# Rounding by an integer tile in place of a large added constant, with the input buffer cut from two to one

## The reference, cut to what matters

```python
xn = layernorm(x)                        # x: [8, 4096, 1024], one batch row a core
x  = x + attn(xn) + ffn(xn)

def activation_quant(x):                 # int8 steps, one scale for each token
    scale = 127.0 / clip(max(abs(x), axis=-1), EPS, None)
    return clip(round(x * scale), -128, 127) / scale
def weight_quant(w):                     # -1, 0 or 1, one scale for the whole weight
    scale = 1.0 / clip(mean(abs(w)), EPS, None)
    return clip(round(w * scale), -1, 1) / scale
def bitlinear(x, w, b):
    return activation_quant(rmsnorm(x)) @ weight_quant(w).T + b
ffn  = lambda x: bitlinear(gelu(bitlinear(x, w1, b1)), w2, b2)
# attn: gated linear attention with decay, 16 heads of 64, then an RMS norm,
# a silu gate and the product with Wo
```

## Time and profile before

| What | Value |
|---|---|
| Median of 3 runs | 6116.22 us (6114.14 to 6116.5) |
| The profiled execution: time | 6119.08 us |
| The profiled execution: span of the slowest core (7) | 6117.5 us |
| Spans of the 8 cores | 6094.9 to 6117.5 us |
| Busy in the span: PE, DVE, ACT, POOL | 3221.6, 1884.1, 1217.1, 155.3 us |
| Chain that ended last: PE, DVE, issue, ACT, DMA, SP's queue | 37%, 24%, 13%, 10%, 9%, 6% |
| Granted TensorE clock, mean of each core | 0.699 to 0.701 of full speed |
| Phase A (from the first chunk to the barrier) | about 225 to 3550 us |
| Phase B's chunks | about 3600 us to the end |

### The profile page before, as it was taken

The page is one execution under the profiler, slowest core; times in us unless marked ns, Lnnn a source line. Parts: engine busy times, 40 slices in busy tenths (PEclk is TensorE's granted clock), DMA queues, the critical chain, the costliest instruction groups (busy, mean ns, idle before and its releaser), DMA issues.

```text
span 6117.5 us, 54514 instructions; the slowest of 8 cores (6094.9 to 6117.5 us)
## 1 busy us (share of the span) xinstructions
PE 3221.6 (53%) x17994; PEld 1767.4 (29%) x17994; DVE 1884.1 (31%) x3739; ACT 1217.1 (20%) x2490; POOL 155.3 (3%) x278
## 2 busy tenths in 40 slices
PE   0266566455555656545544525555555555555556
PEld 0144444333333434333323312222222222222222
DVE  1243443433434343434334312222222222222222
ACT  0111111111111111111111112222222222222222
POOL 0000000000000000000000000000000000000000
PEclk9855655655656555556556568888888888888888
DMA  3110110111111111011111040000000000000000
GB/s 101 57 45 27 46 45 26 57 34 57 34 43 38 33 38 42 29 45 39 31 52 40 26 138 25 25 25 25 24 25 25 24 24 25 25 25 25 25 24 17
DMA packets 109195, 230.68 MB, mean 38 GB/s; under 512 B 53845, under 2 KB 54630, under 8 KB 103798
## 3 DMA queue, kind: packets, MB, share of 16 engines
q1 hardware_dynamic: 91702, 180.74, 9.7%
q0 software_dynamic: 17216, 46.45, 2.1%
HBM read 155.54 MB, written 58.72 MB: 35 GB/s over the span
## 4 chain that ended last, share of the span: by engine, by line
PE 37%; DVE 24%; issue 13%; ACT 10%; DMA 9%; SPq 6%; DVEq 1%; ACTq 0%; POOLq 0%
PE PY L1067 8%; PE PSM L717 6%; SPq L928 4%; DMA WST<-w2t 3%; PE PYW L998 3%; PE PVG L554 3%; ACT HG L958 3%; DVE BPART L963 3%; PE PH L947 2%; PE PSM L721 2%; SPq L149 2%; PE PK L760 2%; DVE PBF L736 2%; DMA WST<-w1t 2%; PE PVG L745 1%
## 5 line engine op out<-in xcount | busy, mean ns | idle before, releaser
L947 PE MATMUL PH<-W1Q,XQF 128*128 128x512 bf16 x2048 | 546.5, 414 | 641.0 <-DMA XQF<-scr_xq 515.9
L1067 PE MATMUL PY<-W2Q,HQF 128*128 128x512 bf16 x2048 | 486.0, 380 | 140.3 <-DVE HQF L1059 121.2
L947 PEld LDWEIGHTS PH<-W1Q,XQF 128*128 128x128 bf16 x2048 | 193.4, 103 | 938.9 <-issue 785.4
L963 DVE TENSOR_REDUCE BPART<-HG 128x1 f32<-128x512 f32 x256 | 175.5, 686 | 911.4 <-ACT HG L958 911.4
L717 PE MATMUL PSM<-UFLAT,ONE 1*128 1x128 f32 x1024 | 405.6, 497 | 0.0
L736 DVE TENSOR_TENSOR PBF<-PQS,EBF 128x128 bf16<-128x128 f32 x512 | 135.8, 291 | 866.8 <-ACT EBF L728 866.1
L728 ACT ACTIVATE EBF<-PSM,WNT 128x128 bf16<-128x128 f32 x512 | 146.5, 368 | 1191.6 <-PE PSM L721 1191.5
L554 PE MATMUL PVG<-WG,XNF 128*128 128x512 bf16 x512 | 179.5, 527 | 345.0 <-DVE VB L547 345.0
L1067 PEld LDWEIGHTS PY<-W2Q,HQF 128*128 128x128 bf16 x2048 | 182.4, 97 | 403.0 <-issue 222.0
L1038 ACT ACTIVATE HG<-HG,c_qs 128x512 f32<-128x512 f32 x256 | 184.8, 722 | 483.3 <-DVE HQS L1046 452.7
L482 PE MATMUL PSM<-WAB,XNF 128*128 128x16 bf16 x256 | 11.6, 174 | 497.1 <-DVE XNF L477 497.1
(11 more groups left out here) (205 smaller groups left out, 4691.6 us busy)
## 6 DMA issues: line engine op xcount, KB each, us to landing
WST<-w1t SPq DMA_DIRECT2D x32, 1024.0 KB, 5.7
WST<-w2t SPq DMA_DIRECT2D x64, 512.0 KB, 3.9
XCH<-x SPq DMA_DIRECT2D x32, 512.0 KB, 6.8
XRES<-x SPq DMA_DIRECT2D x32, 512.0 KB, 5.9
y<-GT SPq DMA_DIRECT2D x32, 512.0 KB, 3.1
scr_xq<-XQB POOLq DMA_DIRECT2D x32, 256.0 KB, 2.3
scr_g<-GB POOLq DMA_DIRECT2D x32, 256.0 KB, 2.3
scr_att<-ATB POOLq DMA_DIRECT2D x32, 256.0 KB, 3.3
```

Source lines behind the costliest of these rows:

```text
L947: fns = [(lambda os=os, kt=kt, pp=pp: lambda e: e.matmul((PH1 if pp == 0 else PH2)[:, 0:512], XQF[:, kt * 128:(kt + 1) * 128], W1Q[:, kt * ...
L963: one("v", (lambda os=os: lambda e: e.reduce_max(out=BPART[:, os:os + 1], in_=HG[:, os * 512:(os + 1) * 512], axis=AX, apply_absolute_valu ...
L1067: lambda e: e.matmul(PY[:, ns * 512:(ns + 1) * 512], HQF[pp][:, i * 128:(i + 1) * 128], W2Q[:, kt * E + ns * 512: kt * E + (ns + 1) * 512] ...
```

## The change

All three places now round by converting to an integer type, and the constant goes.

- In `phaseA_front`, `bq` no longer holds `MAGIC`. In place of the one subtraction into `XQB` there are four copies of half the width: f32 `TRND` to a new int32 tile `XQI5` (128x512), `XQI5` to `XQB`, and the same again for the second half. `XQI5` is one tile, so each copy waits for the one before it.
- In `wq_quant`, ACT writes its scaled piece as int8 into the bytes of `WQP`, no longer in place. DVE reads the int8 piece, multiplies by 1 and takes the minimum into `WST`; the maximum into `WQP` is as before.
- In `phaseB_chunk`, ACT writes its half as int8 into a new tile `HQI8` (128x512), and DVE copies from there to `HQS`.
- `XCH` has one buffer where it had two.

```diff
-    XCH = [sbA(f"XCH{i}", [128, E]) for i in range(2)]
+    XCH = [sbA("XCH0", [128, E])] * 2
...
+    XQI5 = sbA("XQI5", [128, 512], mybir.dt.int32)
...
+    rb["XCH1"] = rb["XCH0"]
...
+    WQI = WQP.bitcast if False else WQP
+    rb["WQI"] = rb["WQP"]
+
     def wq_quant(idx, src, dst_scr, rdst, swc):
...
         one("s", (lambda swc=swc, cw=cw: lambda e: e.activation(
-            out=WST[:, 0:cw], in_=WST[:, 0:cw], func=AF.Copy,
-            scale=COL[swc][:], bias=MAGIC))(),
-            reads=[rwst, rcol[swc]], writes=[rwst])
-        one("v", (lambda cw=cw: ts_(WST[:, 0:cw], WST[:, 0:cw], -MAGIC, 1.0,
-                                    OP.add, OP.min))(),
-            reads=[rwst], writes=[rwst])
+            out=WQP[:].bitcast(mybir.dt.int8)[:, 0:cw], in_=WST[:, 0:cw],
+            func=AF.Copy, scale=COL[swc][:]))(),
+            reads=[rwst, rcol[swc], rb["WQP"]], writes=[rb["WQP"]])
+        one("v", (lambda cw=cw: ts_(WST[:, 0:cw],
+                                    WQP[:].bitcast(mybir.dt.int8)[:, 0:cw],
+                                    1.0, 1.0, OP.mult, OP.min))(),
+            reads=[rb["WQP"], rwst], writes=[rwst])
...
-        one("v", ts_(cl("bq"), cl("nmq"), -1.0, MAGIC, OP.mult, OP.add),
+        one("v", ts_(cl("bq"), cl("nmq"), -1.0, None, OP.mult),
...
-        one("v", (lambda xq=xq: lambda e: e.tensor_scalar(
-            out=xq[:], in0=TRND[:], scalar1=-MAGIC, scalar2=None, op0=OP.add))(),
-            reads=[rb["TRND"]], writes=[rxq])
+        for hf in range(2):
+            one("v", (lambda hf=hf: lambda e: e.tensor_copy(
+                out=XQI5[:], in_=TRND[:, hf * 512:(hf + 1) * 512]))(),
+                reads=[rb["TRND"], rb["XQI5"]], writes=[rb["XQI5"]])
+            one("v", (lambda xq=xq, hf=hf: lambda e: e.tensor_copy(
+                out=xq[:, hf * 512:(hf + 1) * 512], in_=XQI5[:]))(),
+                reads=[rb["XQI5"], rxq], writes=[rxq])
...
+    HQI8 = sbB("HQI8", [128, 512], mybir.dt.int8)
+    rb["HQI8"] = R()
...
                 one("s", (lambda q4=q4, half=half: lambda e: e.activation(
-                    out=HG[:, q4 * 1024 + half * 512:
-                           q4 * 1024 + (half + 1) * 512],
-                    in_=HG[:, q4 * 1024 + half * 512:
-                           q4 * 1024 + (half + 1) * 512],
-                    func=AF.Copy, scale=cl("qs2"), bias=MAGIC))(),
-                    reads=[rb["HG"], rc("qs2")], writes=[rb["HG"]])
-                one("v", (lambda q4=q4, half=half, pp=pp:
-                          lambda e: e.tensor_scalar(
-                              out=HQS[pp][:, 0:512],
-                              in0=HG[:, q4 * 1024 + half * 512:
-                                      q4 * 1024 + (half + 1) * 512],
-                              scalar1=-MAGIC, scalar2=None, op0=OP.add))(),
-                    reads=[rb["HG"], rHq], writes=[rHq])
+                    out=HQI8[:], in_=HG[:, q4 * 1024 + half * 512:
+                                       q4 * 1024 + (half + 1) * 512],
+                    func=AF.Copy, scale=cl("qs2")))(),
+                    reads=[rb["HG"], rc("qs2"), rb["HQI8"]],
+                    writes=[rb["HQI8"]])
+                one("v", (lambda pp=pp: lambda e: e.tensor_copy(
+                    out=HQS[pp][:, 0:512], in_=HQI8[:]))(),
+                    reads=[rb["HQI8"], rHq], writes=[rHq])
```

More of the change, by code:

```diff
@@ L236, in build_program @@
     for name in ["WQw", "WKw", "WVw", "WGw", "WABw", "WSTG0", "WSTG1", "WST",
-                 "WQP", "WABS", "XCH0", "XCH1", "XN32_0", "XN32_1", "XNF",
-                 "TRND", "XQB0", "XQB1", "DUMPa", "DUMPb", "DUMPc",
+                 "WQP", "WABS", "XCH0", "XN32_0", "XN32_1", "XNF",
+                 "TRND", "XQI5", "XQB0", "XQB1", "DUMPa", "DUMPb", "DUMPc",
                  "QF", "QSQ", "QTF", "QTH", "KB", "KHI", "KSQ", "KHF", "KHT",
```

## The result

The changed kernel takes 6215.4 us, the kernel before 6117.6 (medians of 8 runs each). The ratio is 1.0167, 95% interval 1.0156 to 1.0178: slower by 1.7%, 95 to 109 us. The forecast was 82 us more, and its range from 6160 to 6270 us.

A forecast was written before the change was run, and what follows sets the result against it. No engine is near full; the chain of waits bounds the kernel. Front copies 42 us plus weight-piece waits 40 us gave 82 us more, 6201 by the profile and 6198 for the median; range 6160 to 6270 us.

The forecast's parts named there:

- The single file of phase A: Phase A: work runs one after another, so DVE time ahead of VB is time of the kernel.
- Four half copies: Phase A front: four copies for one subtraction, 1.30 us more in each of 32 fronts, 42 us.
- The bound from L1046's row: Integer conversions on DVE: 0.423 us per 128x512 taken from the f32 to bf16 row; no row makes int32 copies faster.
- the double rate: DVE speed of L1046's row, 0.423 us for 512 elements, against 0.686 at the single rate.
- The other estimate from that page: Front copies by 58 cycles plus elements over rate: 0.33 us a half copy, front 32 us; rejected for the rows.
- The wait for the store: Weight pieces: ACT writing WQP waits for the previous piece's store out of it; net 40 us more.
- The maximum's lost wait: Weight pieces: the maximum (L153) no longer waits on the store, 0.07 us in 48 pieces, 3 us saved.
- Phase B and one `XCH`: HQS from int8 and the single x buffer: both taken to cost nothing; HQS bounds from -17 to +34 us.
- rival 4: TensorE's clock: more rest raises the granted clock and gives the added time back, 6116 us; chance 4%.
- the likeliest case: Whole kernel: the forecast sum of 82 us more, chance 68%, own range 6185 to 6212 us.
- int8 at the single rate: DVE reads of int8 in weight pieces and HQS run slower: 34 + 34 us, 6266; chance 11%.

The follow-up runs named there:

- the fillers: Kernel before, with the old subtraction into XQB done two, three or five times; ratios to before 1.0068, 1.0127 and 1.0161.
- e9: e8_both with the int32 copy to XQB moved from DVE to ACT; ratio to before 0.9854.
- e3_phaseb_xch: Kernel before, with only the int8 tile HQI8 in phase B and the single XCH; ratio to before 1.0011.
- e8_both: Changed kernel with int32 TRND, one whole copy to XQB, own int8 tile for weight pieces, one DVE operation for both clamps; ratio to before 0.9896.
- e6: Changed kernel with TRND as an int32 tile and one whole copy to XQB in place of four half copies; ratio to before 1.0086.

## Why the prediction was right, and where it was not

- **The single file of phase A.** Right. Every delay put ahead of `VB` is in the time of chunk 31's `XNF` in full, with what the gate's stretch adds on top: 1.3 us a chunk in the change, 0.8, 1.6 and 3.2 with the fillers, and less 0.86 in e9.
- **Four half copies.** Right: 1.30 us forecast, 1.33 to 1.35 measured as means of the kernels with this front, 41.3 us for 31 fronts. The bound from L1046's row was the right one for all three integer forms. The rule that only place and sizes decide about the double rate (the Trainium skill, VectorE: DVE Perf Modes, What auto-detection actually checks) agrees with the trace now: int8 at 423 ns and int32 at 427 for 512 elements. The other estimate from that page, 32 us for the front, does not: the copies took 0.427 us and not 0.33, and the Trainium skill says itself, below the table that the figure is from (VectorE: DVE Perf Modes, The TRN2 errata), that it comes out too low for a single operation.
- **The wait for the store.** Right in mechanism, and nearly in size: net 40 us forecast, 44 measured for 15 of 16 groups. Two terms were off. The maximum's lost wait (3 us) is made up for by the minimum's new one on the load. And the `w1t` stores landed later than in the trace of before: on core 1 the first of each pair took a mean of 8.6 us for 8.0, the load beside it 6.4 for 5.9, and as a mean of the 8 cores 8.2 for 8.0 and 5.9 for 5.8. In e3_phaseb_xch, where the weights are as before, they take 8.2 and 6.0 as well, so it is a drift that comes without the new weight code; its cause is open.
- **Phase B and one `XCH`.** Right: e3_phaseb_xch. The second load of `x` went out at 240.1 on core 1 and landed after 3.8 us; `x` was first read at 252.2. The prediction had allowed 8.3 us for the landing.
- **What failed: nothing was put down for the clock in the gate's matmuls.** I had the clock as rival 4 with the other sign, priced for all of PE's share of the chain, and read only that two long stages have about the same mean clock. The row that mattered was the short one: 16 matmuls that start at 1.2 GHz after a rest, 5.16 us in the earlier trace rows. Their time depends on when in them the clock rises: 3.86 us at the lower level before, 4.61 after. It cost 11.7 us, most of the 16 by which the sum was short.
- **The range** of the likeliest case, 6185 to 6212, was too narrow for the same reason: 6215 lies 3 us above it. The stated one held, and that is in part luck: its upper end had been set for int8 at the single rate, which did not come, and not for this.
- **Adding parts.** The front alone and the weights alone move chunk 31's `XNF` by 64.9 and 47.3 us, together 112; the change moves it by 97.1. The group and front terms do add; the gate's stretch (14.1 and 1.7 us alone, 11.7 together) and the time ahead of `KB` (2.1 and 0.1, together -3.5) do not.

## What to carry to other kernels

When a scratch tile is used a second time, list what reads it last: a DMA out of it makes the first step of the next round wait where only the last step did, and the price is how much later the store lands than the load, pair by pair. A conversion on the way out of an instruction that is there anyhow cost nothing here (1278 ns to f32 and to int32 on DVE, 722 ns to f32 and to int8 on ACT); a conversion as a copy of its own costs its 0.43 us and a wait of 0.10, and in these runs it paid only where it came with a tile of its own and let two operations become one (e8_both). Where PE starts cold behind a step that is changed, look at how the time of those matmuls spreads over the chunks (here the stretch is 5.3 to 7.0 us): the mean can move within that spread, and it moved by up to 0.45 us in every chunk.

## What the hardware showed beyond that

- The gate's stretch against the delay, 5.94, 6.24, 6.32 to 6.39, 6.38, 5.92, 5.99 us at 0, 0.8, 1.3, 1.6, 3.2, 3.5 us, rises and falls again. Before the stretch PE has rested for 7 to 22 us (means of 10 to 15 us by kernel) and stands at the lower level, and each us that the matmuls run at this level costs 0.46 to 0.50 us, kernel by kernel. The Trainium skill, TensorE: Matmul & The Clock Gate, Part 1, says that when the clock rises depends on where the first matmul lands in a window that runs on by itself and does not start anew with the kernel. The single stretches agree in that they vary (5.3 to 7.0 us in the kernel before). That the mean over 248 stretches moves with the delay is more than this, and that it is 6.05 and 6.14 us in e6 and e8, with no delay, says that the delay is not all. What decides over the mean, no run here shows.
- An ACT instruction that writes int8 takes what it took for f32: the 256 instructions of L1050 above have a mean of 722 ns, and so had those of L1038 before the change, which wrote f32.
- The clock records show a further level beside the two, 0.81, and two cores of a die can be held there far longer than the other two. In e9_act_cast it stands in the clock records of cores 2 and 3 for 1111 us, nearly all of it in phase B, in those of cores 0 and 1 for 335 and 376 us, nearly all in phase A, and in those of cores 4 to 7 not at all. One such stretch, windows view of core 2 (window, length, busy us (count) for five engines, PEclk, DMA share, GB/s):

```profile
4105.00:4139.00 34.00, 22.73 (x104) 9.22 (x101) 8.21 (x15) 4.33 (x6) 0.01 (x1) 0.81 0.00 0
```
